# A two-stage audio kernel on one core: the short filter shared by two engines, TensorE's waits thinned, three steps of the last stage moved

## The reference, cut to what matters

```python
# 1. attention inside each block, softmax(x x^T / 16) x
scores = einsum('bsqd,bskd->bsqk', q, k) * scale
attn = einsum('bsqk,bskd->bsqd', softmax(scores), v)
# 2. a delta-rule mixer on layernorm(h)
q, k, v = (silu(causal_dwconv(x @ W, conv_w)) for each)     # 4 taps
beta = sigmoid(x @ Wb)
delta_out, _ = delta_rule_chunkwise(q, k, v, beta)          # recurrence over chunks
fir_short = causal_dwconv(v, fir_short_w)                   # 3 taps, per channel
fir_long = causal_dwconv(v, fir_long_w)                     # 63 taps
w = softmax(mlp([x, branch statistics of fir_short, fir_long, delta_out, v]) / temp)
o = w0 * fir_short + w1 * fir_long + w2 * delta_out + w3 * v
h = h + (o * rsqrt(mean(o * o)) * o_norm_w) @ Wo
# 3. six experts of 128 hidden units, two of them chosen by a router
h = h + einsum('bteh,ehd,bte->btd', gelu(x @ w1), w2, expert_weights)
```

## Time and profile before

| | us |
|---|---|
| median of 3 runs | 2378.38 |
| lowest and highest run | 2372.26, 2381.79 |
| the profiled execution | 2393.8 |
| its span, first to last instruction | 2392.1 |

### The profile page before, as it was taken

The page is one execution under the profiler, slowest core; times in us unless marked ns, Lnnn a source line. Parts: engine busy times, 40 slices in busy tenths (PEclk is TensorE's granted clock), DMA queues, the critical chain, the costliest instruction groups (busy, mean ns, idle before and its releaser), DMA issues.

```text
span 2392.1 us, 53303 instructions
## 1 busy us (share of the span) xinstructions
PE 2251.9 (94%) x20796; PEld 1635.1 (68%) x20796; DVE 1852.8 (77%) x5111; ACT 1290.8 (54%) x2632; POOL 555.5 (23%) x413
## 2 busy tenths in 40 slices
PE   5999999999799779999999999999999999999997
PEld 4666666666587666777677767776776677767765
DVE  4999999999868367677778777777777667767765
ACT  4888888888624334544454455445544544454452
POOL 1444444444400011121112111111111121112111
PEclk9999999999958879999999999999999999999999
DMA  3776777777778912233224222322233224222300
GB/s 98 231 245 229 229 241 245 236 238 236 247 241 314 378 60 71 71 108 96 78 70 139 91 77 71 125 81 74 70 132 105 71 70 133 77 71 76 125 21 21
DMA packets 224297, 334.44 MB, mean 140 GB/s; under 512 B 113870, under 2 KB 190766, under 8 KB 215342
## 3 DMA queue, kind: packets, MB, share of 16 engines
q1 hardware_dynamic: 219726, 309.01, 39.1%
q10 hardware_dynamic: 2304, 12.58, 1.3%
q0 software_dynamic: 2016, 9.44, 1.0%
HBM read 191.66 MB, written 164.23 MB: 149 GB/s over the span
## 4 chain that ended last, share of the span: by engine, by line
PE 49%; DVE 7%; ACT 6%; issue 4%; POOL 0%; DVEq 0%
PE bank L1662 7%; PE bank L1672 7%; PE bank L1595 6%; PE bank L1475 4%; PE bank L1555 4%; PE bank L1632 4%; PE bank L1571 2%; PE bank L1507 2%; PE bank L1543 2%; ACT L1808 2%; ACT L1803 2%; DVE v_all L2111 1%; PE bank L1503 1%; PE bank L1485 1%; DVE DL L2019 1%
## 5 line engine op out<-in xcount | busy, mean ns | idle before, releaser
L2111 DVE SCALAR_TENSOR_TENSOR v_all<-bank,we,v_all 128x256 f32<-128x256 f32 x576 | 264.9, 476 | 219.3 <-PE bank L1672 214.3
L739 DVE SCALAR_TENSOR_TENSOR Y<-bank,convw,Y 128x383 f32<-128x383 f32 (+2 forms) x576 | 330.6, 602 | 3.2 <-ACT Y L627 2.9
L1672 PE MATMUL bank<-w2e,HE 128*128 128x256 f32 x1152 | 327.9, 395 | 2.4 <-DVE v_all L2111 2.3
L1662 PE MATMUL bank<-v_all,w1e 128*128 128x384 f32 x768 | 289.6, 500 | 2.4 <-ACT HE L1808 2.3
L445 PE MATMUL bank<-pb,wqkv 128*128 128x384 f32 x768 | 282.4, 491 | 1.8 <-DVE Y L739 1.8
L1672 PEld LDWEIGHTS bank<-w2e,HE 128*128 128x128 f32 x1152 | 198.0, 191 | 55.3 <-issue 19.3
L1808 ACT ACTIVATE HE<-bank 128x384 f32<-128x384 f32 x192 | 94.1, 490 | 248.9 <-PE bank L1662 248.2
L1595 PE MATMUL bank<-v_all,w1g 128*128 128x384 f32 x512 | 193.4, 500 | 2.0
L1662 PEld LDWEIGHTS bank<-v_all,w1e 128*128 128x128 f32 x768 | 134.5, 191 | 75.9 <-issue 19.8
L445 PEld LDWEIGHTS bank<-pb,wqkv 128*128 128x128 f32 x768 | 132.1, 191 | 61.1 <-DVE Y L739 8.3
L1786 ACT ACTIVATE first_stage<-bank 32x384 f32<-32x384 f32 (+1 forms) x192 | 92.2, 480 | 135.7 <-PE bank L1583 119.2
(11 more groups left out here) (217 smaller groups left out, 5199.1 us busy)
## 6 DMA issues: line engine op xcount, KB each, us to landing
packa<-pa SPq DMA_DIRECT2D x32, 1932.0 KB, 6.2
v_all<-packa SPq DMA_DIRECT2D x32, 1932.0 KB, 8.1
packb<-pb SPq DMA_DIRECT2D x32, 768.0 KB, 6.1
v_all<-packb SPq DMA_DIRECT2D x32, 768.0 KB, 10.8
toeplitz<-taps SPq DMA_DIRECT2D x128, 190.0 KB, 5.3
toep<-toeplitz SPq DMA_DIRECT2D x32, 760.0 KB, 7.6
packb<-fsk SPq DMA_DIRECT2D x32, 384.0 KB, 2.7
...
```

The costliest lines, as they stand in the source:

```text
L739: dve.scalar_tensor_tensor(out=Y[:, j, lag:T], in0=proj_bank[j][:, 0:T - lag], scalar=convw[:, j, CK - 1 - lag:CK - lag], in1=Y[:, j, lag: ...
L1662: mm = pe.matmul(bank[6][:, 0:T], w1e[:, a, k, :], YT[s][:, a, :], start=(a == 0), stop=(a == HALF - 1))
L1672: pe.matmul(expert_bank(b), HE[k % 2][:, b * P:(b + 1) * P], w2e[:, k, :], start=True, stop=True)\
L2111: dve.scalar_tensor_tensor(out=HA[s][:, b, :], in0=expert_bank(b), scalar=we[s][:, b, k:k + 1], in1=HA[s][:, b, :], op0=ALU.mult, op1=ALU. ...
```

## The change

It has three parts.

1. Short filter, first stage. Channels 128 to 255 (half 1, in the code `a = 1`) stay on VectorE: one product and two taps. Channels 0 to 127 go to GpSimd, which does five operations: the product with w[2] into fsT (`even_first`), and for each of the two other weights a product into a new tile `fir_part` and a sum into fsT (`even_tap`). A new signal `fir_even` counts them, five for each item. TensorE's `fir_to_tokens` waits for `fir_even`, and ScalarE's silu of j = 4 also for the `fir_even` of the item before.
2. Waits of TensorE in the first stage. Stand-alone waits go from 491 to 198 over the stage, about 9 fewer in an iteration.
3. Order of VectorE in the last stage. `delta_out(n, ., 0)` stands before `routing_weights`, `remainder(n, 1)` before `weigh(it, ., 2)`, and `remainder(n, 2)` before `add_expert(e, 1, 0)`.

```diff
...
         eb, b1, kbs = (sb(f"t{n}", [P, NM]) for n in range(3))
+        fir_part = sb("fir_part", [P, T])
         beta = sb("beta", [P, NM])
...
         vtok_copied = signal("vtok_copied")
-        fir_step = signal("fir_step", 6)
+        fir_step = signal("fir_step", 3)
+        fir_even = signal("fir_even", 5)
         fs_copied = signal("fs_copied")
...
                     pe.wait_ge(*xT01_copied.now(n))
-                    pe.wait_ge(*xT2_copied.now(n))
-                    pe.wait_ge(*h_ready.before(n))
                     if n > 1:
                         pe.wait_ge(*hvk_ready.now(n - 2))
+                    else:
+                        pe.wait_ge(*xT2_copied.now(n))
                     for b in range(BLK):
...
                         pe.wait_ge(loaded, 16 * 9)
-                    if j == 0:
+                    if j == 0 and 0 in halves:
                         pe.wait_ge(*xnT0_copied.now(n))
                         pe.wait_ge(*xnT1_copied.now(n))
-                    pe.wait_ge(*(taps_done(n - 1, j + 3) if j < 3 else taps_done(n, j - 3)))
+                    elif 0 in halves:
+                        pe.wait_ge(*(taps_done(n - 1, j + 3) if j < 3 else taps_done(n, j - 3)))
                     for a in halves:
...
 
-                    pe.wait_ge(*sq_ready.now(n))
-                    pe.wait_ge(*h_ready.now(min(n + 1, NB - 1)))
-                    pe.wait_ge(*hvk_ready.before(n))
+                    if 0 in part:
+                        pe.wait_ge(*sq_ready.now(n))
                     for f in part:
...
                 def transpose_head_values(n):
-                    pe.wait_ge(started, 1)
                     pe.wait_ge(*hv_copied.now(n))
...
                 def v_to_tokens(n):
-                    pe.wait_ge(*silu_done.now(n, 6))
                     pe.wait_ge(*ktok_copied.now(n))
...
                 def fir_to_tokens(n):
-                    pe.wait_ge(*fir_step.now(n))
+                    pe.wait_ge(*fir_even.now(n))
                     pe.wait_ge(*vtok_copied.now(n))
...
                     kT, kbT = chans(pa[n % 2], KT), chans(pa[n % 2], KBT)
-                    pe.wait_ge(started, 1)
-                    pe.wait_ge(*kbT0_copied.now(n))
-                    pe.wait_ge(*kbT1_copied.now(n))
+                    if b == 0:
+                        pe.wait_ge(*kbT0_copied.now(n))
+                        pe.wait_ge(*kbT1_copied.now(n))
                     for hh in range(NH // 2):
...
                         act.wait_ge(*fir_step.before(n))
+                        act.wait_ge(*fir_even.before(n))
                         act.wait_ge(*vtok_ready.before(n))
...
 
-                def fir_first(n, a):
-                    dve.wait_ge(*silu_done.now(n, 5 + a))
+                def fir_first(n):
+                    dve.wait_ge(*silu_done.now(n, 6))
                     dve.wait_ge(*fs_ready.before(n))
-                    dve.tensor_scalar(fsT[:, a, :], VT[:, a, :], firw[:, a, FS - 1:FS], None, ALU.mult).then_inc(fir_step.sem, 1)
-
-                def fir_tap(n, a, lag):
-                    dve.wait_ge(*fir_step.now(n, 2 * (lag - 1) + a + 1))
-                    dve.scalar_tensor_tensor(out=fsT[:, a, lag:T], in0=VT[:, a, 0:T - lag],
-                                             scalar=firw[:, a, FS - 1 - lag:FS - lag], in1=fsT[:, a, lag:T],
+                    dve.tensor_scalar(fsT[:, 1, :], VT[:, 1, :], firw[:, 1, FS - 1:FS], None, ALU.mult).then_inc(fir_step.sem, 1)
+
+                def fir_tap(n, lag):
+                    dve.wait_ge(*fir_step.now(n, lag))
+                    dve.scalar_tensor_tensor(out=fsT[:, 1, lag:T], in0=VT[:, 1, 0:T - lag],
+                                             scalar=firw[:, 1, FS - 1 - lag:FS - lag], in1=fsT[:, 1, lag:T],
                                              op0=ALU.mult, op1=ALU.add).then_inc(fir_step.sem, 1)
...
                     if 0 <= c < NB:
-                        fir_first(c, 0)
                         head_sums(c)
-                        fir_first(c, 1)
-                        fir_tap(c, 0, 1)
-                        fir_tap(c, 1, 1)
-                        fir_tap(c, 0, 2)
+                        fir_first(c)
+                        fir_tap(c, 1)
                     if 0 <= b < NB:
...
                     if 0 <= c < NB:
-                        fir_tap(c, 1, 2)
+                        fir_tap(c, 2)
                     if 0 <= b < NB:
...
 
+                def even_first(n):
+                    pool.wait_ge(*silu_done.now(n, 5))
+                    pool.wait_ge(*fs_ready.before(n))
+                    pool.tensor_tensor(fsT[:, 0, :], VT[:, 0, :], firw[:, 0, FS - 1:FS].broadcast_to([P, T]),
+                                       ALU.mult).then_inc(fir_even.sem, 1)
+
+                def even_tap(n, lag):
+                    pool.wait_ge(*fir_even.now(n, 2 * lag - 1))
+                    pool.tensor_tensor(fir_part[:, lag:T], VT[:, 0, 0:T - lag],
+                                       firw[:, 0, FS - 1 - lag:FS - lag].broadcast_to([P, T - lag]), ALU.mult)\
+                        .then_inc(fir_even.sem, 1)
+                    pool.wait_ge(*fir_even.now(n, 2 * lag))
+                    pool.tensor_tensor(fsT[:, 0, lag:T], fsT[:, 0, lag:T], fir_part[:, lag:T], ALU.add).then_inc(fir_even.sem, 1)
+
                 def beta_k(n):
...
                     if 0 <= c < NB:
+                        even_first(c)
+                        even_tap(c, 1)
                         k_norms(c)
+                        even_tap(c, 2)
                         keep_v(c, 0)
...
                         gate_weights(it)
+                    if 0 <= n < NB:
+                        delta_out(n, n % 2, 0)
                     if 0 <= e < NB:
                         routing_weights(e, e % 2)
+                    if 0 <= n < NB:
+                        remainder(n, 1)
                     if 0 <= it < NB:
                         weigh(it, it % 2, 2)
-                    if 0 <= n < NB:
-                        delta_out(n, n % 2, 0)
-                        remainder(n, 1)
                     if 0 <= f < NB:
...
                         mix_add(it, it % 2, 4, tb[:, :].rearrange("p (m d) -> p m d", d=DH))
+                    if 0 <= n < NB:
+                        remainder(n, 2)
                     if 0 <= e < NB:
...
                     if 0 <= n < NB:
-                        remainder(n, 2)
                         delta_out(n, n % 2, 1)
```

## The result

| | before | after |
|---|---|---|
| median, us | 2377.8 (4 runs) | 2397.3 (4 runs) |
| lowest and highest, us | 2372.3, 2381.8 | 2396.2, 2403.0 |
| the profiled execution, us | 2393.8 | 2396.2 |

The changed kernel takes 1.009 times as long, 95% interval 1.007 to 1.011; by the medians it is 19.5 us slower. The forecast was 4.5 us faster.

The account below looks back on a forecast made before the run. The prediction took a 19.2 us first-stage loop through four engines as the bound, VectorE nearly level. Gains of 1.5 us (TensorE's waits) and 3 us (last stage) made 4.5, from 2378.4 to 2374 us, range 2355 to 2390.

Parts of the forecast that it names:

- closed loop: First stage: chain through TensorE, ScalarE, VectorE and GpSimd, 19.2 us by itself, so less filter work on VectorE shortens nothing.
- near-by second limit: First stage: VectorE's 99% busy share limits the iteration at nearly the same height, but is not the only limit.
- two holds of VectorE's filter operations: First stage: GpSimd's filter operations hold VectorE's product 0.55 us and first tap 0.43, eating the 1.39 us removed.
- walk: Step-by-step timing of one iteration's operations; GpSimd filter operations taken at 0.81 us, sums allowed up to 1.0.
- The maximum comes neither earlier nor later.: First stage: the split filter leaves the maximum of the scores unmoved; at 0.9 us an operation, about 0.3 later.
- third rival: First stage: holds push the maximum 0.3 us back every time, 9 us lost, 2384 us; chance 0.15.
- fourth rival: First stage: GpSimd's last sum holds the scaling behind the maximum up to 0.65 us, 20 us lost, 2396; chance 0.10.
- rule of the holds: VectorE and GpSimd operations reading SBUF alone exclude each other; the later waits for the whole of the other.
- TensorE's waits: First stage: about 9 fewer stand-alone waits an iteration gain 0.05 us each iteration, 1.5 us in all, bounds 0 and 4.
- first place: Last stage, TensorE's wait for delta_out ahead of L1543: it goes, but waits for the remainder and w2e piece replace it.
- first rival: Last stage: the first routing product slips in ahead of GpSimd, saving 14 us there, 2360 us; chance 0.17.
- second place: Last stage, TensorE's wait for the remainder ahead of L1555: removing it wins 0.45 us an iteration.

Follow-up runs that it names:

- even_out: Kernel before, with the short filter of half 0 left out on both engines, its result staying zero; 2376.9 us against 2376.1.
- before_shared: Kernel before, with a 128x256 copy moved from ScalarE to VectorE in the first stage; 2383.7 us against 2375.9.
- sum_behind: Changed kernel, with GpSimd's last filter sum made to wait until VectorE's scaling behind the maximum is done; 2377.7 us.
- power_second: Changed kernel, with GpSimd's power between the first and second filter products, its last product and sum behind the scaling; 2369.9 us.
- product_first: Kernel before, last stage reordered: first routing product kept ahead of GpSimd's start, then delta_out, both remainders earlier; 2341.1 us against 2376.1.

## Why the prediction was wrong

**What bounds the kernel.** Right. The closed loop of 19.2 us without a filter operation in it was shown by even_out (19.19), the near-by second limit by before_shared (19.37). What the prediction says would show it, VectorE's share under 95%, did not come: it stayed at 98.3, since the holds count as busy time.

**The two holds of VectorE's filter operations.** Right in kind, near in size: product 0.94 - 0.41 = 0.53 us (0.55 predicted), first tap 1.24 - 0.61 = 0.63 (0.43). The tap's hold came out longer since the sum takes 1.00 us, not 0.81. The prediction allowed sums up to 1.0 and then made its walk with 0.81.

**"The maximum comes neither earlier nor later."** Wrong by a little. The copy of xT stands ahead of the filter in both kernels. Before, it starts at 416.23, and the maximum and its scaling start 19.20 us behind these rows:

```profile
402.54 0.55 DVE L705 TENSOR_REDUCE s<-bank 128x3 f32<-128x384 f32 x1
403.12 0.17 DVE L708 TENSOR_SCALAR s<-s 128x3 f32<-128x3 f32 x1
...
416.23 0.41 DVE L701 COPY xT<-bank 128x256 f32<-128x256 f32 x1
```

From the copy to the maximum it is 402.54 + 19.20 - 416.23 = 5.51 us before, and 400.33 + 20.10 - 414.73 = 5.70 after: 0.19 later. That agrees with the 0.17 us an iteration that sum_behind leaves, 5 us in all, against the 9 of the third rival. So the third rival came in as well, at about half its price.

**The step that failed: the place of GpSimd's last sum.** The fourth rival had the mechanism and the operation and got 0.10, because "by my walk it begins just behind" the scaling. The text's own numbers don't say that. From 416.17, three operations 0.88 apart, the power of 2.3 us and one more product put the last sum at about 422.0; the scaling of the next item is at 403.12 + 19.20 = 422.32. The sum stands ahead of it, and reaches past it by 0.5 us. So the condition "within 0.1 us before the scaling" was too narrow as well: it is the condition for the whole hold, and any sum that still runs holds the scaling for its rest. The walk was ended at the tap and never carried on to the last two of the five operations, and the forecast had no term for them. In the trace after (operations 0.90 apart, the power 2.56 and the maximum 0.19 later) the sum stands 0.11 us ahead of the scaling and the hold is 0.73 us, most of the sum.

That the fourth rival's 2396 fell so near to the measured 2397 is in part luck. By its own terms it is 2378.4 + 20 - 4.5 = 2394 (and the third rival's 2384 is 2383). Measured were 0.73 us of hold instead of 0.65, about 5 us more from the later maximum, and 7 us gained in the last stage instead of 3.

**The rule of the holds.** It was taken too widely: "two operations that read SBUF alone exclude each other". The power let VectorE's taps through (power_second), and a reduction and a reciprocal ran inside GpSimd's product. For the operations of this forecast, products, sums and the scaling, it held.

**TensorE's waits.** Right as far as it can be seen: 0.04 us an iteration in the profile, 0.05 predicted; the time shows nothing.

**The last stage.** The walk held at the first place: the first routing product was held until 1265.06, GpSimd's first product having ended at 1265.03, and TensorE's wait for delta_out gave way to one for the remainder (0.44 us) and one at the expert's piece (0.16). The first rival (the product slips in) fell. The second place was worth 0.56 us where I had 0.45, and the other half of the order cost 0.38, as the walk had it (0.35 to 0.45). So the gain was 0.18 an iteration instead of 0.10, 6 to 7 us instead of 3. The most that both places together could give was put at 33 us; product_first got 35.

## What to carry to other kernels

An engine at 99% may have a loop of equal length beside it: leave its work out once and look whether the time moves, before any of it is paid for elsewhere. When work goes to GpSimd, write down for every one of its products and sums, to the last, which VectorE operation on SBUF alone asks for access while it runs; a small one on the critical path can pay most of the length of a large one. Where such a pair falls together, try an order or a wait that puts the small one first: here one wait gave back 20 us of the changed kernel, and the last stage's order with its first routing product ahead of GpSimd's start made the kernel before 35 us faster.
